# Handing the last stores of two projections to the stages behind them, in a two-layer graph network on one core

## The chip, the cores and the metric

The kernel runs on one core of a Trainium2 chip. Its time is the device time of one execution in microseconds (us), and the median of several runs is compared. Engines are named as in the profile: PE is TensorE (PEld its weight loads), DVE is VectorE, ACT is ScalarE, POOL is GpSimd and SP is SyncE, which only issues DMAs.

## The reference

There are N=1250 nodes with 768 features, 20,000 edges and a loop at each node. Two layers are computed, each with a residual and a layer norm.

```python
# layer 0: x -> x2
x1 = relu(x @ W_ah + b_ah)
for W, a_s, a_d, b in three_convs:          # 4 heads of 192 each: 12 heads in all
    h = (x1 @ W).reshape(N, 4, 192)
    e = leaky_relu((h*a_s).sum(-1)[src] + (h*a_d).sum(-1)[dst], 0.2)
    p = exp(e - segment_max(e, dst)[dst])
    xs.append(relu(segment_sum(p/(segment_sum(p, dst)[dst]+1e-16) * h[src], dst) + b))
x2 = layernorm(x + relu(concat(xs) @ W_out + b_out))

# layer 1: x2 -> out
h   = elu(gat(x2, W1, heads=4, width=512) + b1)
out = layernorm(x2 + gat(h, W2, heads=1, width=768) + b2)
```

## The kernel before

Edges are turned into a dense 1250x1250 matrix of counts (CT), so that an aggregation is a dense product. With u and v, two numbers per destination, the weight of a pair is `min(max(exp(src+u), exp(0.2*src+v)), 1) * CT`. Nodes stand in NT=10 tiles of T=125. The program is eight stages, each a block in which every engine has its own written list of instructions. A block ends when all its engines have ended, with a barrier, and semaphores are cleared behind it.

1. `counts_and_x1`: counts CT, the mask G, and x1, split into two rounded parts (x1T). At its end stands TensorE's `turn_row`, ScalarE's last `mask`.
2. `project` (h of layer 0). VectorE rounds the score weights (wa_hi, wa_lo, L741 and L743); TensorE forms the 24 rows of scores with them (L833, fp32r); ScalarE copies the rows (L788), stores them to DRAM (L791) and fetches the rows of heads 0 and 1 back, each broadcast to 125 partitions (`src_row`, L794). Then TensorE runs 60 tiles of products (L855, six units of ten tiles) and ScalarE keeps each tile in `h_out` (L818), which SP stores to `h_rows` half a unit at a time. Beside it VectorE takes 120 maxima, one for each head and tile (L756), each over a broadcast row; SP fetches the row of a later head into the buffer that has fallen free, in one queue with the stores. From the maxima come u and v of all heads. They are turned by TensorE one after the other (L863), with a copy by ScalarE between and behind (L823), and stored by SP for heads 4 to 11 (L719). SP ends when all stores of h and of u and v have landed. The first head's u, v and h are loaded ahead, into `first_room`.
3. `aggregate_layer0`: six iterations of two heads, ten steps each. A step is two exps by ScalarE (L1002), a maximum and a product with CT by VectorE (L1040, L1045), and ten fp32 products by TensorE (L1089). VectorE also reduces chunks of w2 into score weights in steps 4, 11 and so on; GpSimd loads them (L579, L583). `tail_room`, with the turned results, is allocated here.
4. `project_out_layer0`: ScalarE rounds chunks of W_out (L1770) as they land, VectorE takes the rest (L1808), TensorE multiplies (L1882) and VectorE and ScalarE normalize tile by tile.
5. `project_layer1`: x2 is turned (L1350) and split, products in eight units (L1375), each tile kept as a rounded part by ScalarE (L1268) and the rest by VectorE (L1333) in `h_out`, stored half a unit at a time, tiles 5 to 9 first. SP ends when all stores have landed.
6. `aggregate_layer1`: 120 steps over four heads and three thirds of the destinations. A step is two exps (L1531), maximum and product (L1581, L1583), p rounded (`round_p`, L1503) and its rest (`rest_of_p`, L1573), and 14 products (L1639, L1619). ScalarE first rounds the ones and the negated bias (L1493, L1495). h comes in one load of 0.51 MB per tile. ELU at the end of each third.
7. `project_out_layer1`: chunks of W2 and pieces of the turned result (`f_raw`) are loaded, rounded (L1994, L2002), and multiplied (L2121).
8. `aggregate_last`: 20 steps, with h rounded (L2219) and split (L2248) beside the first ten, then the last layer norm.

```python
            for h in range(2):     # L793, ScalarE in project
                dma_in_two(act, src_row[:, h, :], score_rows[h:h + 1, :].broadcast_to([T, N]), row_in[h])
```

## Time and profile before

| | |
|---|---|
| median of 3 runs | 1965.33 us (1964.57 to 1966.22) |
| the profiled execution | 1964.74 us, span of its instructions 1963.0 us |
| TensorE, VectorE, ScalarE, GpSimd busy | 93%, 74%, 53%, 7% of the span |
| mean granted TensorE clock | 0.968 of full speed |

The span runs from the first to the last instruction. The clock has two levels, 2.4 GHz (1.00 in the views) and 1.2 GHz (0.50). A busy TensorE is not one at its peak, since matrix products are pipelined. Idle time of an engine that doesn't set the end costs nothing.

### The profile page before, as it was taken

Reading aid. Unit: us, or ns where it says so; the run is one execution under the profiler, and the core shown is the slowest. Engines: PE = TensorE matmul, PEld = TensorE weight load, DVE = VectorE, ACT = ScalarE, POOL = GpSimd, SP = SyncE. Lnnn points to the kernel's source line nnn. Section 1 sums busy time; section 2 is a strip of 40 time slices with the busy share of each in tenths; the row PEclk is TensorE's granted clock in tenths of the full one; section 3 lists DMA queues with packets and bytes.
Section 4 is the critical chain, followed back from the end, with each engine's and each line's share of the span. In section 5 each row is a group of like instructions: output and inputs, shape, how many; then the busy total and the mean of one; then the engine's idle time right before and its main releaser. Section 6 shows DMA issues by size and latency. Waiting matters only on the chain. (4 is left out here: it accounts for less than half of the span.)

```text
span 1963.0 us, 30340 instructions
## 1 busy us (share of the span) xinstructions
PE 1817.6 (93%) x11217; PEld 1754.5 (89%) x11217; DVE 1445.3 (74%) x2468; ACT 1034.1 (53%) x1631; POOL 135.3 (7%) x132
## 2 busy tenths in 40 slices
PE   7999899995999999997999899969999996999898
PEld 5777689995999999996999799969999996999798
DVE  7787659998989988984555559447888885346756
ACT  3666522215798898875211322257788874232633
POOL 5011022110000000000011011100000000000000
PEclk8999999997999999997999999989999998999899
DMA  4122154445284344537654566472342406545302
GB/s 123 52 62 67 35 154 138 116 118 133 62 210 100 100 110 101 132 72 197 182 172 147 143 188 192 141 190 66 118 140 68 133 27 183 166 122 129 101 9 79
DMA packets 181465, 234.72 MB, mean 120 GB/s; under 512 B 76102, under 2 KB 154288, under 8 KB 181083
## 3 DMA queue, kind: packets, MB, share of 16 engines
q1 hardware_dynamic: 173215, 205.31, 38.1%
q0 software_dynamic: 7216, 24.91, 4.4%
q10 hardware_dynamic: 902, 2.72, 0.5%
q8 instruction: 85, 1.39, 0.3%
q14 instruction: 47, 0.39, 0.1%
HBM read 167.89 MB, written 65.00 MB: 119 GB/s over the span
## 5 line engine op out<-in xcount | busy, mean ns | idle before, releaser
L1639 PE MATMUL p_o<-p_hi,h_parts 125*128 125x416 f32 (+1 forms) x960 | 282.7, 355 | 22.0 <-DVE p_lo L1573 15.5
L1089 PE MATMUL p_o<-first_room,p 125*125 125x193 f32 x1200 | 202.7, 330 | 13.2 <-DVE p L1045 10.4
L1089 PEld LDWEIGHTS p_o<-first_room,p 125*125 125x125 f32 x1200 | 197.9, 190 | 14.8 <-issue 14.3
L1639 PEld LDWEIGHTS p_o<-p_hi,h_parts 125*128 125x128 f32 x960 | 181.7, 189 | 28.2 <-issue 15.7
L1089 PE MATMUL p_o<-h_in,p 125*125 125x193 f32 x1200 | 198.1, 327 | 0.8 <-ACT res L976 0.8
L1089 PEld LDWEIGHTS p_o<-h_in,p 125*125 125x125 f32 x1200 | 196.0, 188 | 2.3 <-ACT res L976 1.2
L756 DVE CUSTOM_DVE_ANT_0 max_junk<-src_row,G 125x1250 bf16<-125x1250 f32 x120 | 186.2, 1623 | 9.9 <-DMA src_row<-score_rows 9.3
L1040 DVE TENSOR_TENSOR e<-e 125x1250 f32<-125x1250 f32 x120 | 174.3, 1452 | 20.0 <-ACT e L1002 19.9
L855 PE MATMUL p_h<-pw_hi,x1T 128*125 128x384 f32 x720 | 186.4, 340 | 0.0
L1045 DVE SCALAR_TENSOR_TENSOR p<-e,CT 125x1250 f32<-125x1250 f32 x120 | 175.3, 1461 | 4.1
L1375 PE MATMUL p_h<-pw_hi,x2T 128*125 128x256 f32 (+1 forms) x960 | 173.1, 282 | 0.0
L1639 PE MATMUL p_o<-p_lo,h_parts 125*128 125x416 f32 (+1 forms) x480 | 169.9, 354 | 0.0
L1002 ACT ACTIVATE e<-first_room,col 125x1250 f32<-125x1250 f32 x120 | 151.0, 1345 | 7.2 <-DMA b_col<-in_b_gat 4.4
L1002 ACT ACTIVATE e<-uv,col 125x1250 f32<-125x1250 f32 x120 | 149.1, 1349 | 0.9 <-DVE p L1045 0.9
L1375 PEld LDWEIGHTS p_h<-pw_hi,x2T 128*125 128x125 f32 x960 | 146.8, 186 | 0.0
L1375 PE MATMUL p_h<-pw_lo,x2T 128*125 128x256 f32 (+1 forms) x480 | 135.0, 281 | 0.0
L450 PE MATMUL p_count<-src_hot,dst_hot 125*125 125x416 bf16 (+1 forms) x588 | 116.0, 354 | 17.1 <-ACT dst_hot L347 11.3
L855 PEld LDWEIGHTS p_h<-pw_hi,x1T 128*125 128x125 f32 x720 | 130.7, 187 | 0.1
L1882 PE MATMUL p_y<-fw_hi,f_hi 128*125 128x384 f32 x360 | 122.9, 341 | 7.2 <-DVE fw_lo L1808 7.1
L2121 PE MATMUL p_y<-fw_hi,f_hi 128*125 128x386 f32 x320 | 110.6, 346 | 18.1 <-DVE fw_lo L2032 14.6
L450 PEld LDWEIGHTS p_count<-src_hot,dst_hot 125*125 125x125 bf16 x588 | 81.0, 142 | 51.4 <-ACT dst_hot L347 15.5
L278 DVE TENSOR_SCALAR src_hot<-node_no,edge_col 125x1250 bf16<-125x1250 int16 x196 | 106.3, 572 | 27.3 <-PE p_count L450 24.8
(255 smaller groups left out, 3863.3 us busy)
## 6 DMA issues: line engine op xcount, KB each, us to landing
f_raw<-turned SPq DMA_DIRECT2D x40, 500.0 KB, 8.8
h_rows<-h_out SPq DMA_DIRECT2D x32, 560.0 KB
h_parts<-h_rows SPq DMA_DIRECT2D x40, 448.0 KB
turned<-tail_room SPq DMA_DIRECT2D x18, 625.0 KB, 7.3
G<-turned SPq DMA_DIRECT2D x20, 562.5 KB
h_rows<-h_out SPq DMA_DIRECT2D x24, 424.4 KB
first_room<-in_w_gat POOLq DMA_DIRECT2D x36, 192.0 KB, 2.7
first_room<-in_w_gat SPq DMA_DIRECT2D x6, 1152.0 KB
```

The lines of the kernel that those rows point to most:

```text
L278: hot = v.tensor_scalar(src_hot[:, h, :], node_no[:], edge_col[:, 0, h, at], None, ALU.is_equal)
L450: last = nc.tensor.matmul(p_count[:, i, 0:w], dst_hot[:, h, :], src_hot[:, h, a:a + w], start=False, stop=False, skip_group_check=True)
L756: v.tensor_tensor_reduce(out=junk[:, t % 2, :], in0=src_row[:, h % 2, :], in1=G[:, t, :], scale=1.0, scalar=NO_EDGE, op0=ALU.subtract, op1 ...
L855: last = nc.tensor.matmul(p_h[:, (u * NT + t) % 4, 0:width], xp[:, k, at], wp[:, u, k, :], start=(k == 0 and n == 0), stop=(k == KD - 1 an ...
L1002: last = a.activation(e[:, g % RING, kind, :], uv[hh][:, kind, :], ACT.Exp, bias=col_src[kind][:, bass.ds(i * 2 + hh, 1), s])
L1040: v.tensor_tensor(e[:, g % RING, 0, :], e[:, g % RING, 0, :], e[:, g % RING, 1, :], ALU.max).then_inc(more_ready, 1)
L1045: v.scalar_tensor_tensor(p[:, g % RING, :], e[:, g % RING, 0, :], 1.0, CT[:, s, :], ALU.min, ALU.mult).then_inc(p_ready, 1)
L1089: last = nc.tensor.matmul(p_o[:, b, n * 256:n * 256 + C0 + 1], p[:, g % RING, d * T:(d + 1) * T], h_in[hh][:, s, 0:C0 + 1], start=(s == 0 ...
L1375: last = nc.tensor.matmul(p_h[:, n % 4, 0:width], xp[:, k, at], wp[:, q % 2, k, 0:width], start=(k == 0 and j == 0), stop=(k == KD - 1 and ...
L1639: last = nc.tensor.matmul(p_o[:, bank(n, c), 0:w], h[:, s, kind, cols].bitcast(F32R), pp[:, g % RING, 0:w], start=(s == 0 and j == 0), sto ...
L1882: last = nc.tensor.matmul(p_y[:, t % 2, half, 0:CW], fp[:, n % 2, kk, :], wp[:, k, cols], start=(k == 0 and j == 0), stop=(k == KO - 1 and ...
L2121: last = nc.tensor.matmul(p_y[:, t % 2, 0:CW + 2], fp[:, m % 2, kk, :], wp[:, k, :], start=(k == 0 and j == 0), stop=(k == K1 - 1 and j == 2))
```

## The change

- `project`: the score weights are rounded at the end of stage 1 (the room comes from smaller constants there). TensorE itself spreads head 0's score row over 125 partitions, as a product of a column of the identity with the rows, and ScalarE copies it; head 1's row still comes by DMA. `h_out` and `turned_uv` lie in `tail_room`, which is allocated before this stage now. The last half unit of h and the late u and v are not stored here, and nobody waits for landings. u and v are turned in one go.
- `aggregate_layer0`: GpSimd issues the two stores of u and v and the four of h first, then its weight loads. Waits for them stand where their data is first read or their room first written. The wait for the bias moves to where it is used.
- `project_layer1` and `aggregate_layer1`: the same for the last half unit of h (tiles 0 to 4 of the last 256 columns), with four DMAs by GpSimd. An exp in the projection loads the table ahead. The rounding of the ones and of the bias goes behind the first and the fourth step's exps.
- `aggregate_last`: step 0's exps go ahead of the rounding of h, and step 0's p is split at once.
- Identity products by TensorE (`keep_busy`) at ends and starts of stages.

```diff
+def keep_busy(nc, ident, out, n):
+    for _ in range(n):
+        nc.tensor.matmul(out, ident[:, 0:out.shape[0]], ident[:], start=True, stop=True)
 # counts_and_x1: VectorE's end, TensorE's end
+            dve.wait_ge(weighed.summed, weighed.chunks * 2 * weighed.heads)
+            v.tensor_copy(wa_hi[:], wa_flat).then_inc(wa_rounded, 1)
+            dve.wait_ge(wa_rounded, 1)
+            v.tensor_tensor(wa_lo[:], wa_flat, wa_hi[:].bitcast(F32), ALU.subtract)
+            keep_busy(nc, ident, p_count[:, 0, 0:128], 8)
 # project, SyncE
                     for part_no in range(2):
+                        if (i, u, part_no) == (iters - 1, 1, 1):
+                            break
                         wait_apart(sp, h_kept, i * (2 * NT) + (NT * u + NH * (part_no + 1) + 4))
...
-            for u in range(2):
-                sp.wait_ge(h_stored[u], 32 * per * (2 * iters + 1))
-            for kind in range(2):
-                sp.wait_ge(uv_kept, kind + 1)
-                sp.dma_start(core.uv_rows[kind, HG * NT:heads * NT, :], turned_uv[HG * NT:, kind, :]).then_inc(uv_stored, 16)
-            sp.wait_ge(uv_stored, 32)
 # project, ScalarE
             act.dma_start(score_rows[0:R, :], rows[:]).then_inc(rows_stored, 16)
+            act.wait_ge(row_spread, 1)
+            for b, (at, n) in enumerate(CH):
+                last = a.activation(src_row[:, 0, at:at + n], p_r[0:T, b, 0:n], ACT.Copy)
+            last.then_inc(row_in[0], 32)
             act.wait_ge(rows_stored, 16)
-            for h in range(2):
-                dma_in_two(act, src_row[:, h, :], score_rows[h:h + 1, :].broadcast_to([T, N]), row_in[h])
+            dma_in_two(act, src_row[:, 1, :], score_rows[1:2, :].broadcast_to([T, N]), row_in[1])
...
-            for kind in range(2):
-                act.wait_ge(uv_turned, kind + 1)
-                a.activation(turned_uv[:, kind, :], p_s[0:heads * NT, 0:T], ACT.Copy).then_inc(uv_kept, 1)
+            act.wait_ge(uv_turned, 1)
+            a.activation(turned_uv, p_s[0:heads * NT, 0:2 * T].rearrange("p (a q) -> p a q", a=2), ACT.Copy)
 # project, TensorE
-            pe.wait_ge(wa_split, 1)
...
             last.then_inc(rows_turned, 1)
+            for b, (at, n) in enumerate(CH):
+                last = nc.tensor.matmul(p_r[0:T, b, 0:n], ident[0:R, 0:1].broadcast_to([R, T]), rows[:, at:at + n],
+                                        start=True, stop=True)
+            last.then_inc(row_spread, 1)
 # aggregate_layer0: GpSimd, SyncE, ScalarE, TensorE
+            for kind in range(2):
+                pool.dma_start(core.uv_rows[kind, H0 * NT:2 * ITERS * NT, :], uv_last[H0 * NT:, kind, :]).then_inc(core.uv_late, 16)
+            for g in range(2):
+                dma_in_two(pool, h_rows[2 * ITERS - 2 + g, DH:, :].rearrange("(t p) c -> p t c", p=T), h_last[:, 1, :, g, :],
+                           core.h0_late)
...
+            for stored_h in core.h0_stored:
+                sp.wait_ge(stored_h, all_h - 64)
             load(0)
...
+                if i == 0:
+                    sp.wait_ge(core.uv_late, all_uv)
+                if i + 2 == ITERS - 1:
+                    sp.wait_ge(core.h0_stored[0], all_h)
+                    sp.wait_ge(core.h0_late, 64)
                 load(i + 2)
...
-            act.wait_ge(bias_in, 16)
...
+            keep_busy(nc, ident, p_t[:, 0, 0:128], 12)
...
             for c in range(CW):
                 turn(ITERS - 1, c)
+            keep_busy(nc, ident, p_o[:, 0, 0:128], 6)
 # project_out_layer0, TensorE: at the start, and at the end
+            keep_busy(nc, core.ident, p_y[:, 1, 0, 0:128], 7)
...
+            pe.wait_ge(y_left, 2 * (NT - 1))
+            keep_busy(nc, core.ident, p_y[:, NT % 2, 0, 0:128], 28)
 # project_layer1: SyncE, ScalarE
+                    if (q, n) == (UNITS - 1, 1):
+                        break
...
-            for part in range(2):
-                sp.wait_ge(h_stored[part], 64 * UNITS)
...
+                if n == 2 * NT:
+                    a.activation(table_ahead[:], ident[0:T, 0:1], ACT.Exp)
 # aggregate_layer1: GpSimd, SyncE, ScalarE, TensorE
+            for kind in range(2):
+                dma_in_two(pool, h_rows[H1 - 1, 0:DH, kind, HALF1:].rearrange("(t p) c -> p t c", p=T),
+                           h1_last_part(core)[:, :, kind, :], core.h1_late)
...
+            for stored_h in core.h1_stored:
+                sp.wait_ge(stored_h, 64 * (UNITS - 1))
             for s in range(NT):
                 load_h(0, s)
...
-            act.wait_ge(ones_set, 1)
-            a.activation(ones[:], ones_f[:], ACT.Copy).then_inc(ones_set, 1)
-            act.wait_ge(bias_in, 16)
-            a.activation(b_minus[:], b_col[:], ACT.Copy, scale=-1.0).then_inc(bias_in, 16)
-            act.wait_ge(bias_in, 32)
...
+                if g == 0:
+                    act.wait_ge(ones_set, 1)
+                    a.activation(ones[:], ones_f[:], ACT.Copy).then_inc(ones_set, 1)
                 if g:
                     round_p(g - 1)
+                if g == 3:
+                    act.wait_ge(bias_in, 16)
+                    a.activation(b_minus[:], b_col[:], ACT.Copy, scale=-1.0).then_inc(bias_in, 16)
+                    act.wait_ge(bias_in, 32)
...
-            pe.wait_ge(ones_set, 2)
+            keep_busy(nc, core.ident, p_o[:, 7, 0:128], 9)
...
+            pe.wait_ge(left, (ENDS - 1) * CW)
+            keep_busy(nc, core.ident, p_o[:, bank(ENDS - 2, CW - 1), 0:128], 40)
 # project_out_layer1, TensorE's start
+            keep_busy(nc, core.ident, p_y[:, 1, 0:128], 11)
 # aggregate_last: ScalarE, VectorE, TensorE
-                if part == 0:
-                    a.activation(h_hi[:, s, :], h2[:, s, :], ACT.Copy).then_inc(h_hi_done, 1)
+                if part == 0 and s > 1:
+                    round_h(s)
...
-                if g:
+                if g == 0:
+                    round_h(0)
+                    round_h(1)
+                    round_p(0)
+                if g > 1:
                     round_p(g - 1)
...
-                if part == 0:
+                if part == 0 and s:
                     rest_of_h(s)
...
-                if g and s != 1:
+                if g == 0:
+                    rest_of_h(0)
+                    rest_of_p(0)
+                elif s != 1:
                     rest_of_p(g - 1)
                 add(g)
-                if s == 1:
+                if g == NT + 1:
                     rest_of_p(g - 1)
...
+            keep_busy(nc, core.ident, p_o[:, 7, 0:128], 16)
```

## Rows read from the trace of the kernel before

**Rows 1.** The page: busy time of the engines, and two of its groups.
```profile
PE 1817.6 (93%) x11217; PEld 1754.5 (89%) x11217; DVE 1445.3 (74%) x2468; ACT 1034.1 (53%) x1631; POOL 135.3 (7%) x132
...
L1089 PE MATMUL p_o<-h_in,p 125*125 125x193 f32 x1200 | 198.1, 327 | 0.8 <-ACT res L976 0.8
...
L756 DVE CUSTOM_DVE_ANT_0 max_junk<-src_row,G 125x1250 bf16<-125x1250 f32 x120 | 186.2, 1623 | 9.9 <-DMA src_row<-score_rows 9.3
```

**Rows 2.** Waits of TensorE over the span: us in total, times, longest.
```profile
PE p_o L1639 <- DVE p_lo L1573: 15.5, 1, 15.5
PE p_y L2121 <- DVE fw_lo L2032: 14.6, 1, 14.6
...
PE p_o L1089 <- DVE p L1045: 10.4, 1, 10.4
```

**Rows 3.** Timeline of the first projection's start: start, length, idle time before.
```profile
251.44 2.13 ACT L785 ACTIVATE pw_hi<-first_room 128x2304 fp32r<-128x2304 f32 x1 [1.90 <-DMA first_room<-in_w_gat]
...
254.91 1.31 ACT L788 ACTIVATE score_rows_in<-p_r 24x418 f32<-24x418 f32 x3 [1.34 <-PE p_r L833]
...
256.27 1.27 PE L838 MATMUL p_s<-ident,score_rows_in 24*125 24x24 f32 x10 [1.40 <-ACT score_rows_in L788]
...
261.29 1.91 ACTq L93 DMA_DIRECT2D src_row<-score_rows  x4
...
269.42 1.46 DVE L756 CUSTOM_DVE_ANT_0 max_junk<-src_row,G 125x1250 bf16<-125x1250 f32 x1 [9.29 <-DMA src_row<-score_rows]
```

**Rows 4.** Timeline from the projection's end into the first aggregation, all engines.
```profile
448.62 0.34 PE L855 MATMUL p_h<-pw_hi,x1T 128*125 128x384 f32 x1
...
458.82 0.19 DVE L769 SCALAR_TENSOR_TENSOR col<-dst_now,tmp 125x40 f32<-125x40 f32 x1
...
463.26 0.36 SPq L925 DMA_DIRECT2D b_col<-in_b_gat  x1
...
465.14 6.25 ACT L1002 ACTIVATE e<-first_room,col 125x1250 f32<-125x1250 f32 x5 [4.41 <-DMA b_col<-in_b_gat]
...
484.22 0.72 POOL L583 DMA_DIRECT2D wa_by_w<-in_w  x1 [18.29 <-DVE wa L597]
```

**Rows 5.** Windows where TensorE starts: busy us (instructions) by engine, granted clock, DMA.
```profile
470.80:475.80 5.00, 5.00 (x16) 5.00 (x17) 4.93 (x4) 5.00 (x5) 0.00 (x0) 0.50 1.01 283
475.90:480.90 5.00, 5.00 (x33) 5.00 (x32) 4.93 (x5) 5.00 (x5) 0.00 (x0) 1.00 0.72 159
...
1304.70:1308.70 4.00, 4.00 (x12) 3.81 (x13) 3.90 (x8) 4.00 (x9) 0.00 (x0) 0.50 1.05 261
...
1837.60:1841.20 3.60, 3.59 (x17) 3.60 (x18) 3.56 (x5) 3.11 (x5) 0.00 (x0) 0.50 0.38 109
```

**Rows 6.** Timeline from layer 1's projection into its aggregation.
```profile
1289.61 0.42 DVE L1333 TENSOR_TENSOR h_out<-p_h,h_out 125x256 fp32r<-125x256 f32 x1 [1.70 <-ACT h_out L1268]
...
1297.04 0.36 SPq L1467 DMA_DIRECT2D b_col<-in_b  x1
...
1299.16 1.28 ACT L1531 ACT_TABLE_LOAD   x1
...
1303.94 0.59 DVE L1573 TENSOR_TENSOR p_lo<-e,p_hi 125x418 fp32r<-125x418 f32 x1
```

**Rows 7.** Timeline of ScalarE at the start of the two output projections.
```profile
916.04 0.85 ACT L1770 ACTIVATE fw_hi<-G 128x768 fp32r<-128x768 f32 x1 [1.86 <-DMA G<-in_w_out]
...
1658.50 1.04 ACT L2002 ACTIVATE f_hi<-f_raw 128x1000 fp32r<-128x1000 f32 x1 [4.87 <-DMA f_raw<-turned]
```

**Rows 8.** Timeline of the last aggregation's start.
```profile
1829.52 0.84 ACT L2219 ACTIVATE h_hi_l<-h 125x768 fp32r<-125x768 f32 x1 [8.87 <-PEq L69]
1830.27 1.51 ACT L2223 ACTIVATE G<-x_ring,col 125x625 f32<-125x625 f32 x2
...
1831.81 0.81 DVE L2314 TENSOR_TENSOR G<-G 125x625 f32<-125x625 f32 x1 [0.46 <-ACT G L2223]
...
1837.61 0.97 PE L2347 MATMUL p_ol<-h_hi_l,p_hi_l 125*125 125x256 f32 x3 [9.62 <-DVE p_lo_l L2252]
```

More of the change, by code:

```diff
@@ L217, in _ @@
                                pattern=[[1, NT]], channel_multiplier=-1).then_inc(later_ready, 1)
-            for m in (band, ident_b, zeros_b):
-                pool.memset(m[:], 0.0).then_inc(consts, 1)
-            pool.wait_ge(consts, 6)
-            pool.affine_select(out=ident_b[:], in_=ident_b[:], compare_op=ALU.not_equal, fill=1.0, base=0,
-                               pattern=[[-1, T]], channel_multiplier=1).then_inc(consts, 1)
+            pool.memset(band[:], 0.0).then_inc(consts, 1)
+            pool.wait_ge(consts, 4)
             pool.affine_select(out=band[:], in_=band[:], compare_op=ALU.not_equal, fill=1.0, base=N - T,
@@ L251, in _ @@
             step(v.scalar_tensor_tensor(meets[:, 0, :], least, tile_lo[:, 1:2], meets[:, 0, :], ALU.is_lt, ALU.mult))
-            step(v.scalar_tensor_tensor(meets[:, 1, :], run_no_i[:], float(-ER), meets[:, 0, :], ALU.add, ALU.mult))
-            step(v.scalar_tensor_tensor(meets[:, 2, :], run_no_i[:], 1.0, meets[:, 0, :], ALU.add, ALU.mult))
+            step(v.scalar_tensor_tensor(meets[:, 1, :], run_no_i, float(-ER), meets[:, 0, :], ALU.add, ALU.mult))
+            step(v.scalar_tensor_tensor(meets[:, 2, :], run_no_i, 1.0, meets[:, 0, :], ALU.add, ALU.mult))
             step(v.tensor_reduce(out=range_f[:, 2:3], in_=meets[:, 1, :], axis=AX.X, op=ALU.min))
@@ L452, in count @@
                         last.then_inc(hot_free, 1)
-                nc.tensor.matmul(p_count[:, 0, 0:2], zeros_b[:], band[:, 0:2], start=False, stop=True,
+                nc.tensor.matmul(p_count[:, 0, 0:2], zeros_b, band[:, 0:2], start=False, stop=True,
                                  skip_group_check=True).then_inc(counted, 1)
@@ L653, in project @@
         h_kept = sem("h_kept")
-        h_stored = [sem(f"h_stored{u}") for u in range(2)]
+        h_stored = core.h0_stored
         ones_set = sem("ones_set")
@@ L787, in _ @@
             for b, (at, n) in enumerate(CH):
-                last = a.activation(rows[:, at:at + n], p_r[:, b, 0:n], ACT.Copy)
+                last = a.activation(rows[:, at:at + n], p_r[0:R, b, 0:n], ACT.Copy)
             last.then_inc(rows_kept, 1)
@@ L981, in keep @@
             def keep(i, c):
+                if i == 0 and c == 0:
+                    act.wait_ge(bias_in, 16)
+                    act.wait_ge(core.uv_late, all_uv)
+                    act.wait_ge(core.h0_stored[0], all_h)
+                    act.wait_ge(core.h0_late, 64)
                 act.wait_ge(turned, i * CW + (c + 1 + CW))
@@ L1157, in project_layer1 @@
         h_split = sem("h_split")
-        h_stored = [sem(f"h_stored{u}") for u in range(2)]
+        h_stored = core.h1_stored
         uv_turned = sem("uv_turned")
@@ L1443, in bank, with _ @@
             return (n * PER + c) % 8
+        UNITS = 2 * H1
+        @block.gpsimd
+        def _(pool):
+            for kind in range(2):
+                dma_in_two(pool, h_rows[H1 - 1, 0:DH, kind, HALF1:].rearrange("(t p) c -> p t c", p=T),
+                           h1_last_part(core)[:, :, kind, :], core.h1_late)
         @block.sync
@@ L1510, in elu_exp @@
                 act.wait_ge(left, k)
+                if n == 0 and c == 0:
+                    act.wait_ge(core.h1_late, 64)
                 if n >= 2:
@@ L2421, in gnn_two_layers @@
             core.first_h_in = sem0("first_h_in")
+            core.h0_stored = [sem0(f"h0_stored{u}") for u in range(2)]
+            core.uv_late = sem0("uv_late")
+            core.h0_late = sem0("h0_late")
             with ExitStack() as inner:
@@ L2437, in gnn_two_layers @@
             tail.close()
-            with ExitStack() as innermost:
-                sb2 = core.tools(innermost)[0]
-                x2T = [sb2(f"x2T{i}", [128, KD, N], F32R) for i in range(2)]
-                project_layer1(nc, core, x2T, x2_rows, w1, core.wa1, h1_rows, score_rows, cols[0:2], *cols[2:4])
-            w2_halves = w2.rearrange("(u g) r c -> u (g r) c", u=2)
-            with ExitStack() as ahead:
+            with ExitStack() as ahead:
+                core.tail_room = ahead.enter_context(nc.sbuf_tensor("tail_room1", [128, TAIL1], F32, side="right"))
+                core.h1_stored = [sem1(f"h1_stored{u}") for u in range(2)]
+                core.h1_late = sem1("h1_late")
+                with ExitStack() as innermost:
+                    sb2 = core.tools(innermost)[0]
+                    x2T = [sb2(f"x2T{i}", [128, KD, N], F32R) for i in range(2)]
+                    project_layer1(nc, core, x2T, x2_rows, w1, core.wa1, h1_rows, score_rows, cols[0:2], *cols[2:4])
+                w2_halves = w2.rearrange("(u g) r c -> u (g r) c", u=2)
                 core.f_raw = ahead.enter_context(nc.sbuf_tensor("f_raw", [128, 2, K1 // 2, T], F32, side="right"))
                 core.w_first = ahead.enter_context(nc.sbuf_tensor("fw_first", [128, K1 // 2, D // 2], F32, side="right"))
-                core.tail_room = ahead.enter_context(nc.sbuf_tensor("tail_room1", [128, TAIL1], F32, side="right"))
                 aggregate_layer1(nc, core, h1_rows, cols[0:2], b1, turned1, w2_halves)
```

82 lines of the change are left out of this document (46 added, 36 removed).

## The prediction, made before the changed kernel was run

> **What bounds the kernel now.** I read the page first. TensorE is busy for 93% of the span, VectorE for 74% [rows 1]: time is to be won where TensorE stands still or runs at half clock. The waits of TensorE, sorted by length, come next. Eight of them, from 4.6 to 15.5 us, happen once each, at or near a border between two stages; three stand here [rows 2]. Then I took the timeline at each border and asked what ends last.
>
> In the first projection that is not TensorE. Its last product starts at 448.62, while VectorE ends its chain of maxima at 459.01 [rows 4]. That chain starts at 269.42 behind 9.3 us of waiting for the first broadcast row of scores, and 9.9 us is all the idle time its 120 maxima have [rows 1, 3]. So it moves as a block: a start x earlier is an end x earlier.
>
> **The change part by part.** The sum is made in the profiled execution: span 1963.0, its time 1964.74. The median of the runs is 1965.33, and I subtract the sum from that.
>
> *First row by TensorE.* ScalarE rounds the second weights until 251.44+2.13=253.57 [rows 3]. TensorE's score products, freed from a wait for VectorE at the stage's start, are done by about then. So: three copies 1.31, to 254.9; ten transposes 1.27, to 256.2 [rows 3]; then the new spread, three fp32 products of 418 columns, which run as two passes each (L1089 stands with 2,400 instructions for 1,200 products). A pass of 193 columns takes 198.1/1200=0.165 us [rows 1], and twice that at half clock, where 5 us hold 16 passes for 33 [rows 5]; times 418/193 and six passes that is 2.1 or 4.3 us. Three copies of 125 partitions: at least the 1.31 of the copies of 24, I take 1.4. With the hand-overs the maxima start at 259.9 to 262.1; I take the middle, 261.0, a shift of 8.4, so the chain ends at 450.6. TensorE's own products start at 258.3 to 260.5, up to 3 us later than now, and end at 448.3 to 451.9, beside the chain. The other rows are issued when a buffer falls free; a row is then wanted ten maxima of 1.46 us later, and the first two took 8.1 us from their issue at 261.29 [rows 3]. That slack hides them.
>
> *Last stores handed over.* From the chain's end to the next stage's first issue it takes 4.25 us, 459.01 to 463.26 [rows 4], for two transposes, two copies, a store of u and v, its landing and the barrier. After: two transposes without a copy between (0.6 with the hand-over), one copy (0.4, as one of the three above), 1.0 for barrier and clearing. That is 452.6 for 463.26: 10.6 gained with the 8.4.
>
> *GpSimd's six issues.* They stand ahead of the weight loads that VectorE first reduces in step 4, some 18 us into the stage. An issue cost 0.72 us beside running VectorE products [rows 4]; a store of h has 2.2 times as many pieces as that load, so 0.72 to 1.6 each, 4.3 to 10 us in all, and the load lands in time. Cost 0, hidden by four steps. The Trainium skill (SBUF — State Buffer, 🔬 SBUF: two separate sides) speaks against handing DMAs to GpSimd: while VectorE runs certain two-port copies, GpSimd can't write descriptors, and a DMA goes from about 0.62 to 3.1 us. By that, as an estimate, six issues take some 19 us and VectorE would wait a few us once. The 0.72 us row does not show it for the products that run here.
>
> *First aggregation, start.* The first exps no longer wait for the bias: 465.14 [rows 4] for 463.5, 1.6. Then 5.66 us of exp, maximum and product remain to TensorE's start at 470.80 [rows 5]. TensorE's first 5 us ran at half clock: 2.5 lost [rows 5]. The stage is TensorE's from its first step (20 passes, 3.3 us, against two VectorE products of 1.46), so clock is time here. The 12 identity products are 24 passes of 128 columns, 0.11 us at full and 0.22 at half by the same rows: 2.6 or 5.2 us, under the cover of those 5.66. They leave up to 3 us of idle before the real products, so I take half of the 2.5: 1.3 (0 to 2.5). This border: 10.6+1.6+1.3=13.5.
>
> *Output projection of layer 0.* Its start at half clock returns nothing: the ninth weight chunk reaches ScalarE only at 916.04 [rows 7] and TensorE about 1.8 later (0.85 for the rounding, as much for the rest), when it is about there now; a faster TensorE waits for the DMA. The six products behind the last turn may pass the barrier: -0.1 (0 to -0.5).
>
> *Projection of layer 1, start.* ScalarE and VectorE round and subtract in a chain that TensorE's transposes only follow: 0.2.
>
> *Second aggregation, start.* The last subtraction ends at 1290.03, the next stage begins at 1297.04 [rows 6]. Without the landing of the last stores 1.0 of barrier is left: 6.0 gained. Then the table load of 1.28 goes [rows 6] (into the projection, on a ScalarE that waits for TensorE at every tile), with the rounding of the ones and the wait for the bias. Exps could begin at 1297.35 and p_lo be ready at 1301.8; now 1303.94+0.59=1304.5: 2.7. Its first 4 us at half clock [rows 5] cost up to 2.0. Against that stands a transfer that used to be over: 1.28 MB of stores now share the engines with ten loads of 0.51 MB, and the engines are already full at 261 GB/s [rows 5]. A load takes 2.0 us of it, TensorE's step 2.7. If the store goes first it costs 1.28/0.261=4.9 us, of which the loads' lead hides 1.3 by the third step: up to 3.6. The larger pieces of the loads should get more than half: I take 1.8 for contention, and 0.4 of the clock. The Trainium skill (DMA: Bandwidth & Descriptors, Issuing engines are not separate DMA queues) says that transfers issued by different engines interleave on the same 16 engines; by that GpSimd's queue gives no room of its own, and the sum would carry the full 3.6. This border: 6.0+2.7+0.4-1.8=7.3 (4.5 to 10.7).
>
> *Output projection of layer 1.* Its start at half clock returns nothing either: the third piece is held by a landing at 1658.50 [rows 7], and two faster pieces wait longer for it. 0. The 40 products end 9 to 10 us after the last real one, under the 11 us to the next stage.
>
> *Last aggregation.* Exps first, h rounded behind. From 1829.52: exps 1.51, VectorE's two products 0.81 each [rows 8], p rounded 0.7, then h_lo 0.95 and p_lo 0.8 (by their columns): TensorE starts at 1834.4 for 1837.61 [rows 8]. Step 1 now waits for p_lo(1), behind add(1) and the products of step 2: 1840.8. Before, 17 of step 0's 45 products took 3.6 us at half clock [rows 5], and step 1 began near 1844.4. Gain 3.6 with the clock held, 3.0 without: 3.4.
>
> Sum: 13.5-0.1+0.2+7.3+3.4=24.3. 1965.3-24.3=1941.0.
>
> **Rivals.**
> - *The identity products don't hold the clock.* For: idle stretches of 2 us and more remain between them and the first real products. Against: they halve every stretch. Price 1.3+0.4+0.4: 1943.1.
> - *The late stores take the loads' place.* Full 3.6 for 1.8, and as much again if the loads of the first aggregation are held: 1942.8 to 1945.
> - *The maxima start no earlier,* because the next row is late: all 8.4 lost, 1949.4. For: the first two rows took 8.1 us together. Against: only one is needed now, with ten maxima of cover.
> - *Slower.* GpSimd's issues in the first aggregation. At 8 us each the weight loads land after 50 us, VectorE stands at its first reduction from 18 us on, TensorE behind it, and some 30 us go. It decides from about 7 us each (42 us less 18 eat the 24); at 9 us each it would be 1971. Against: 0.72 us [rows 4].
>
> **How the numbers follow.** Forecast 0.60; clock 0.13; stores 0.13; maxima 0.07; slower 0.03; 0.04 for more than all the bounds. Bounds summed: best 1.1+2.5+3.4+0.5 more than mine, 1933.5; worst -1.5-1.8-2.8-0.9 and the maxima, 1950. The range of 1932 to 1950 leaves out the slower rival and the rest. No change can't be told from differences under 0.2% (3.9 us): faster 0.95, same 0.02, slower 0.03.
>
> **What would show it.** The first maximum a good us behind the score copies instead of 9; the first aggregation beginning near 452.6; no table load in the second, its first product within 5 us of the stage's start or held by h_parts; a wait of TensorE of about 1 us before step 1 of the last stage; longer waits for the DMA in both output projections. I am wrong if VectorE idles between maxima, if TensorE's products end far behind the chain, or if one GpSimd issue is long.

## The result, and the profile after

The change makes the kernel faster. The median of 4 runs is 1947.15 us (1945.75 to 1952.59), against 1965.78 us (1964.57 to 1969.89) in 4 runs of the kernel before: a ratio of 0.9902, 95% interval 0.9882 to 0.9921. The profiled execution has a span of 1944.2 us, for 1963.0 before. That is 18.8 us less, where 24.3 were forecast.

The page first. TensorE is busy for 95% of the span and not 93%, with 280 more instructions (274 passes of identity products and the six of the spread), so that a part of the 95% is no work; the idle time ahead of the maxima has fallen from 9.9 us [rows 1] to 3.2.

```profile
PE 1848.0 (95%) x11497; PEld 1783.2 (92%) x11497; DVE 1445.9 (74%) x2468; ACT 1033.4 (53%) x1634; POOL 140.8 (7%) x139
...
L1118 PE MATMUL p_o<-h_in,p 125*125 125x193 f32 x1200 | 199.8, 329 | 2.8 <-ACT res L1000 2.8
...
L761 DVE CUSTOM_DVE_ANT_0 max_junk<-src_row,G 125x1250 bf16<-125x1250 f32 x120 | 184.9, 1612 | 3.2 <-ACT src_row L799 1.6
```

The waits of TensorE (total, times, longest). The three long ones of [rows 2] are gone from the list, in part only because identity products now stand in them. What is left at the borders is under 3 us each. The wait for ScalarE's `res` inside the first aggregation has grown: in the kernel before its longest was 1.0 us, the first of these rows, and now it is 2.8.

```profile
PE p_o L1089 <- ACT res L976: 3.7, 4, 1.0
```

```profile
PE p_o L1118 <- ACT res L1000: 5.7, 4, 2.8
...
PE p_s L844 <- ACT score_rows_in L793: 1.6, 1, 1.6
```

The start of the first projection, which answers to [rows 3]. The first maximum starts at 262.07 instead of 269.42, behind ScalarE's copy of the spread row and no longer behind a DMA. But the six spreading passes took 4.51 us, all at half clock.

```profile
250.17 10.10 POOL L742 TENSOR_TENSOR pw_lo<-first_room,pw_hi 128x2304 fp32r<-128x2304 f32 x2 [9.07 <-ACT pw_hi L790]
...
254.39 1.67 PE L844 MATMUL p_s<-ident,score_rows_in 24*125 24x24 f32 x10 [1.61 <-ACT score_rows_in L793]
...
255.89 4.51 PE L847 MATMUL p_r<-score_rows_in,ident 24*125 24x418 f32 x6
...
256.54 3.82 DVE L752 COPY col<-score 125x120 f32<-125x120 f32 x1
...
260.33 0.68 PE L865 MATMUL p_h<-pw_hi,x1T 128*125 128x384 f32 x1
...
262.07 1.46 DVE L761 CUSTOM_DVE_ANT_0 max_junk<-src_row,G 125x1250 bf16<-125x1250 f32 x1 [1.58 <-ACT src_row L799]
```

```profile
core 0: us, PE busy (x) PEld busy (x) DVE busy (x) ACT busy (x) POOL busy (x), PEclk, DMA share, GB/s
255.90:260.30 4.40, 4.40 (x7) 1.77 (x7) 4.17 (x3) 0.00 (x0) 4.38 (x1) 0.50 0.83 246
497.50:500.80 3.30, 3.30 (x10) 3.30 (x11) 3.27 (x3) 3.30 (x9) 0.00 (x0) 0.50 1.03 259
1101.70:1105.20 3.50, 1.51 (x6) 1.08 (x6) 3.23 (x5) 1.95 (x5) 0.00 (x0) 0.50 1.02 296
```

The columns of these windows are those of [rows 5]; the value ahead of the DMA share is the granted clock, 0.50 in all three. From the projection's end into the aggregation, for [rows 4]: VectorE is done with the last of the columns at 451.35, but TensorE's own products now last until 452.57, so it is TensorE that ends the stage.

```profile
451.16 0.19 DVE L774 SCALAR_TENSOR_TENSOR col<-dst_now,tmp 125x40 f32<-125x40 f32 x1
...
452.24 0.33 PE L865 MATMUL p_h<-pw_hi,x1T 128*125 128x384 f32 x1
...
453.00 0.37 ACT L830 ACTIVATE tail_room<-p_s 120x250 f32<-120x250 f32 x1
454.16 0.36 SPq L943 DMA_DIRECT2D b_col<-in_b_gat  x1
...
454.63 8.71 ACT L1030 ACTIVATE e<-first_room,col 125x1250 f32<-125x1250 f32 x7 [1.25 <-DVEq L1048]
454.65 1.06 POOL L928 DMA_DIRECT2D uv_rows<-tail_room  x2 [51.12 <-POOLq L70]
...
455.70 2.80 POOL L94 DMA_DIRECT2D h_rows<-tail_room  x4
```

TensorE's and VectorE's rows in the first aggregation show the new wait. TensorE runs the first head's ten steps (200 passes) in 34.40 us, then stands for 2.78 us. VectorE waits 0.88 us for the first weight chunk in step 4; at step 11 two reductions stand ahead of the sums that the divisors are made from.

```profile
460.29 34.40 PE L1118 MATMUL p_o<-first_room,p 125*125 125x193 f32 x200 [2.82 <-issue]
497.47 2.91 PE L1118 MATMUL p_o<-h_in,p 125*125 125x193 f32 x8 [2.78 <-ACT res L1000]
```

```profile
472.53 0.96 DVE L614 CUSTOM_DVE_ANT_1 wa_by_junk<-wa_by_w,wa_by_a 128x768 bf16<-128x768 f32 x1 [0.88 <-DMA wa_by_w<-in_w]
...
494.37 0.95 DVE L614 CUSTOM_DVE_ANT_1 wa_by_junk<-wa_by_w,wa_by_a 128x768 bf16<-128x768 f32 x1
...
496.12 0.16 DVE L1057 TENSOR_SCALAR sums<-p_o 125x4 f32<-125x4 f32 x1
```

Layer 1, for [rows 6]: from the last subtraction to the first issue it takes 0.88 us for 7.01. No table is loaded in the new stage, and `p_lo` is ready 4.2 us into it. TensorE is then held by the load of h, once at its first and once at its third step.

```profile
1283.50 0.42 DVE L1366 TENSOR_TENSOR tail_room<-p_h,tail_room 125x256 fp32r<-125x256 f32 x1 [1.69 <-ACT tail_room L1298]
1284.80 0.36 SPq L1509 DMA_DIRECT2D b_col<-in_b  x1
...
1285.30 2.83 POOL L94 DMA_DIRECT2D h_rows<-tail_room  x4 [35.44 <-POOLq L70]
...
1288.44 0.59 DVE L1623 TENSOR_TENSOR p_lo<-e,p_hi 125x418 fp32r<-125x418 f32 x1
...
1289.66 0.72 PE L1692 MATMUL p_o<-p_hi,h_parts 125*128 125x418 f32 x1 [2.57 <-DMA h_parts<-h_rows]
...
1295.22 0.46 PE L1672 MATMUL p_o<-p_hi,ones 125*128 125x418 f32 x1 [1.24 <-DMA h_parts<-h_rows]
```

To see where the time came from, I cut the span of each execution at the same work: the last product of the counts, the first product of the first aggregation, and the last real product of each stage behind it. Gains are in us against the profiled execution of the kernel before. The last column gives the lowest and highest gain over the nine later kernels that keep the change's identity products, less those whose edit is in that stage.

| part | forecast | after | others |
|---|---|---|---|
| counts | 0 | 0.84 | 0.3 to 2.4 |
| projection, up to the first product of the aggregation | 12.2 | 9.66 | 8.4 to 9.9 |
| first aggregation | 1.3 | -2.63 | -2.8 to -1.7 |
| output projection of layer 0 | -0.1 | -0.57 | -4.5 to 0.0 |
| projection of layer 1 | 0.2 | -1.21 | -2.5 to -1.1 |
| second aggregation with its border | 7.3 | 8.03 | 5.5 to 8.8 |
| output projection of layer 1 | 0 | 1.07 | -1.9 to 2.5 |
| last aggregation | 3.4 | 3.64 | 1.6 to 3.6 |
| sum | 24.3 | 18.8 | |

### The profile page after: what moved, and what is told of

Its sections match the earlier page's. It is cut to its first block and busy times, and to the rows that moved or that the text cites. A ratio compares the mean times of both kernels' runs of the same rounds, so it can differ in the third digit from the quotient of the medians.

```text
span 1944.2 us, 30898 instructions
## 1 busy us (share of the span) xinstructions
PE 1848.0 (95%) x11497; PEld 1783.2 (92%) x11497; DVE 1445.9 (74%) x2468; ACT 1033.4 (53%) x1634; POOL 140.8 (7%) x139
## 5 line engine op out<-in xcount | busy, mean ns | idle before, releaser
L1692 PEld LDWEIGHTS p_o<-p_hi,h_parts 125*128 125x128 f32 x960 | 181.6, 189 | 14.9 <-DVE z L1611 10.2
L865 PE MATMUL p_h<-pw_lo,x1T 128*125 128x384 f32 x360 | 122.4, 340 | 0.0
```

The source lines that it names most:

```text
L865: last = nc.tensor.matmul(p_h[:, (u * NT + t) % 4, 0:width], xp[:, k, at], wp[:, u, k, :], start=(k == 0 and n == 0), stop=(k == KD - 1 an ...
L1692: last = nc.tensor.matmul(p_o[:, bank(n, c), 0:w], h[:, s, kind, cols].bitcast(F32R), pp[:, g % RING, 0:w], start=(s == 0 and j == 0), sto ...
```

## Experiments

Each kernel is the changed one with the edit shown; in a diff, `...` or a comment stands for lines that are not printed. A profile is of one execution, and a median of four or five runs still moves by some 2 us, so a verdict on a part is read from the parts of the profile.

**The changed kernel again**

> The changed kernel once more, for the spread of its stages between executions. If the stages between the borders repeat to 0.3 us and only the half-clock stretches behind waits differ, its parts are as before but for those: 1945 to 1949.

Measured: 1948.21 us (1945.20 to 1950.76), ratio 0.990 (0.9885 to 0.9914), span 1946.5. The projection gains 9.80, the first aggregation -2.55, the second 8.03, as before. The others moved by 0.8, 1.2 and 0.5 us. So the two parts in which most of the forecast is missing repeat. What happens inside the aggregation does not repeat: the weight chunk came 1.4 us later, TensorE waited 3.56 us at the second head, and the clock did not fall there.

```profile
473.96 0.96 DVE L614 CUSTOM_DVE_ANT_1 wa_by_junk<-wa_by_w,wa_by_a 128x768 bf16<-128x768 f32 x1 [2.46 <-DMA wa_by_w<-in_w]
...
498.90 0.40 PE L1118 MATMUL p_o<-h_in,p 125*125 125x193 f32 x1 [3.56 <-ACT res L1000]
```

**Divisors ahead of the reductions**

```diff
-                    if (i * STEPS + g) % 7 == 4 and ...:   # weighed.reduce
-                    if g == NT + 1:
-                        divisors(i, 0)
+                    if g == NT + 1:
+                        divisors(i, 0)
+                    if (i * STEPS + g) % 7 == 4 and ...:   # weighed.reduce
```

> Theory (VectorE's written order makes the wait at the second head of the first aggregation: the divisors stand behind two reductions of 0.95 us, and the idle time then costs a step at half clock): the sums come 1.75 us sooner, TensorE's wait of 2.78 us shrinks to about 1, the next step takes 3.5 us for 5.17; 3.5 us together, 1943.6. Rival (the half clock there has nothing to do with the length of that wait): the step still takes 5.2 us, 1.8 us gained, 1945.4. Rival (the first weight chunk's late landing is the cause): the wait keeps over 2 us, 1946.5 or more.

Measured: 1945.94 us (1944.63 to 1953.64), ratio 0.9906 (0.9889 to 0.9922). The median doesn't resolve it, the profile does: the aggregation as a whole loses 0.78 and not 2.63. The first sums are formed at 494.85, before TensorE has ended the head (496.77), the second head starts at once, and no clock falls. This is the theory's mechanism, but not its 3.5 us: 1.85 are gained, for at the third head TensorE now waits 1.01 us for VectorE's next divisors, a wait that the changed kernel does not have there. The profiled span of 1952.0 is longer all the same. The loss lies elsewhere: the second aggregation began with 10.2 us at half clock for 3.4, the output projection of layer 0 lost 1.6 more, and the last two stages gained 3.0 and 2.0 less.

```profile
494.85 0.16 DVE L1057 TENSOR_SCALAR sums<-p_o 125x4 f32<-125x4 f32 x1
...
497.12 0.96 DVE L614 CUSTOM_DVE_ANT_1 wa_by_junk<-wa_by_w,wa_by_a 128x768 bf16<-128x768 f32 x1
...
529.31 0.15 DVE L1057 TENSOR_SCALAR sums<-p_o 125x4 f32<-125x4 f32 x1
...
530.66 1.05 PE L1118 MATMUL p_o<-first_room,p 125*125 125x193 f32 x5 [1.01 <-ACT res L1000]
```

```profile
496.61 3.64 PE L1118 MATMUL p_o<-h_in,p 125*125 125x193 f32 x20
```

**Weight loads ahead of the late stores**

```diff
-            # GpSimd: two stores of u and v, four of h
             weighed.loads(pool, ...)      # first vector, first two chunks
+            # here the six stores, then the rest of the loads
```

> GpSimd issues its first loads of weights ahead of the six late stores. Theory (the stores only cost VectorE its 0.88 us of waiting for the first chunk): that wait goes, TensorE's wait at the second head shrinks from 2.78 to 1.9 us, and 1.0 us is gained if the clock still falls there, 2.6 if it doesn't: 1946.2 to 1944.5. Rival (what comes late is the traffic of this stage's own loads, whatever the order of issue): no change, 1947.1.

Measured: 1949.16 us (1943.82 to 1951.69), ratio 0.992 (0.9896 to 0.9944). VectorE's wait for the chunk is gone, and the aggregation loses 1.67 for 2.63: 0.96 gained, as the theory has it for a clock that still falls. It did fall (it was down from 496.2 to 499.6). TensorE ran its first head wholly at full clock, came sooner and waited 3.30 us. The profiled execution lost 4.45 us in the output projection of layer 0, with a wait of 4.1 us for a weight chunk and 6.8 us at half clock behind it; against stages that vary so much the median says nothing on this edit.

```profile
496.07 4.20 PE L1122 MATMUL p_o<-h_in,p 125*125 125x193 f32 x14 [3.30 <-ACT res L1004]
```

**No identity products**

```diff
 def keep_busy(nc, ident, out, n):
-    for _ in range(n):
-        nc.tensor.matmul(out, ident[:, 0:out.shape[0]], ident[:], start=True, stop=True)
+    return
```

> All identity products left out. By the prediction's clock terms (1.3, 0.4 and 0.4) it takes 2.1 us more than with them: 1949.3. Rival from the changed kernel's trace (held over the border of the second projection, the clock falls 1.6 us into it instead, and one step of the first aggregation is at half clock behind a wait in either case): 1 us or less, 1948. Rival (the stages' starts are mostly half clock without them, at up to 2 us each at five places): 1952 or more.

Measured: 1943.99 us (1940.40 to 1946.69), ratio 0.9892 (0.9872 to 0.9912). All three expectations were of a longer time; it was not longer. The half-clock stretches between 200 and 1925 us do grow, from 47.8 to 95.6 us in all. What counts is how much of TensorE's real work lies in them, and that grows from 39.9 to 56.7 us only. In the first aggregation those 5 us are at half clock again, but TensorE then comes later to the second head, waits 1.42 us and keeps its clock: the stage loses 0.91 for 2.63.

```profile
458.70:463.70 5.00, 5.00 (x16) 5.00 (x17) 4.93 (x4) 5.00 (x5) 0.34 (x1) 0.50 1.05 297
```

```profile
458.66 35.67 PE L1117 MATMUL p_o<-first_room,p 125*125 125x193 f32 x200 [7.54 <-DVE p L1072]
495.75 3.50 PE L1117 MATMUL p_o<-h_in,p 125*125 125x193 f32 x20 [1.42 <-ACT res L999]
```

**First row by DMA again**

```diff
-            act.wait_ge(row_spread, 1)
-            # three copies from p_r to src_row[:, 0]
             act.wait_ge(rows_stored, 16)
-            dma_in_two(act, src_row[:, 1, :], ...)
+            for h in range(2):
+                dma_in_two(act, src_row[:, h, :], ...)
-            # TensorE: the three products that spread the row
```

> The first broadcast row by DMA again. Theory (the maxima are a rigid chain and the row's 6.5 us pass on, less the 1.2 us by which TensorE's products outlast them in the changed kernel): the first maximum at about 268.6 instead of 262.1, the next stage's first issue 5.3 us later, 1952.4. Rival (TensorE's products set the end of that stage, and starting them 3 us sooner makes up for much of it): under 3 us, 1950 at most.

Measured: 1951.55 us (1951.18 to 1956.06), ratio 0.9936 (0.9919 to 0.9952), some 3 to 4 us more than with the spread. The projection gains 6.37 for 9.66, so the spread is worth 3.3 us of the 8.4 forecast. A part of those came without it: the first maximum started at 266.33, 2.4 us sooner than in [rows 3] beside the 0.7 of the earlier counts. The score weights rounded a stage ahead are the likely cause; no run has that change alone. TensorE's products ended at 448.65, before the maxima, and didn't set the end. The next stage issued at 457.59, 3.4 us later than in the changed kernel and not the theory's 5.3, so the rival is the nearer one on the mechanism, and that the median lies near the theory's 1952.4 is chance.

```profile
266.33 1.46 DVE L761 CUSTOM_DVE_ANT_0 max_junk<-src_row,G 125x1250 bf16<-125x1250 f32 x1 [5.74 <-DMA src_row<-score_rows]
```

**Layer 0's late stores waited for**

```diff
-                        if (i, u, part_no) == (iters - 1, 1, 1):
-                            break
+            # SyncE, at the end of project, behind the last half unit of h: u and v
+            for u in range(2):
+                sp.wait_ge(h_stored[u], 32 * per * (2 * iters + 1))
+            for kind in range(2):
+                sp.dma_start(core.uv_rows[kind, HG * NT:heads * NT, :], turned_uv[...]).then_inc(core.uv_late, 16)
+            sp.wait_ge(core.uv_late, 32)
-            # GpSimd, in aggregate_layer0: the same stores
```

> The last half unit of h and the late u and v of layer 0 are stored and waited for in the projection again. By the prediction's step (store, landing and copy of u and v are some 2 of the 10.6 us): the next stage's first issue 2 us later, 1949. Rival (with TensorE's last product now at the very end, the last half unit of h, 0.96 MB, lands after u and v and holds the stage): 5 to 6 us later, 1952.7. Rival (the first aggregation waits at its second head anyway, so the loads and VectorE's first reduction gain what is lost): 1948 or less.

Measured: 1954.23 us (1950.96 to 1955.67), ratio 0.9932 (0.9909 to 0.9956), 6 to 7 us more than the changed kernel: the first rival's. The stores of h, issued at 448.50, hold u and v until 454.58, and the next stage issues at 457.53. From the last maximum to VectorE's first operation of the aggregation it takes 13.2 us for 6.8, and 9.65 in the kernel before, where the maxima outlasted those stores. So the gain of the row isn't there to be added up without the hand-over: here the spread ran at full clock and the maxima started 10.4 us sooner than in the kernel before (8.1 beside the earlier counts), and yet the projection gains only 4.91. With the hand-over and without the row it gains 6.37, with both 9.66. Both single kernels keep the smaller edits of the change (score weights ahead, one turn for u and v, the bias waited for later), so 4.91 and 6.37 are not the prices of the two parts by themselves.

```profile
448.11 0.19 DVE L779 SCALAR_TENSOR_TENSOR col<-dst_now,tmp 125x40 f32<-125x40 f32 x1
...
448.50 2.52 SPq L94 DMA_DIRECT2D h_rows<-tail_room  x4
...
454.58 0.79 SPq L733 DMA_DIRECT2D uv_rows<-tail_room  x2
457.53 0.36 SPq L943 DMA_DIRECT2D b_col<-in_b_gat  x1
```

**Layer 1's late stores waited for**

```diff
-                    if (q, n) == (UNITS - 1, 1):
-                        break
+            # SyncE, at the end of project_layer1
+            for part in range(2):
+                sp.wait_ge(h_stored[part], 64 * UNITS)
-            # GpSimd, in aggregate_layer1: the four stores
```

> The last half unit of layer 1 is stored and waited for in its projection again. Theory (the landing wait is worth 6.1 us, and the handed-over stores delay the loads by little, about 1 us): from the last subtraction to the next stage's first issue 7.0 us instead of 0.9, loads of h 2.0 us apart from the first, 5 us lost in all, 1952. Rival (the handed-over stores take the loads' place in full, 3.6 us): 2.5 us lost, 1949.6.

Measured: 1952.19 us (1948.30 to 1955.28), ratio 0.9916 (0.9888 to 0.9944), as the theory has it. The border grows from 0.88 to 6.91 us, and the second aggregation with it gains 4.87 for 8.03: 6.0 lost and 2.9 had back. Of these, 1.2 us are the wait at the third step, which is gone, and some 1.5 the half clock, which ended at 1296.5 here, ahead of the first product (1297.87).

```profile
1285.72 0.42 DVE L1366 TENSOR_TENSOR tail_room<-p_h,tail_room 125x256 fp32r<-125x256 f32 x1 [1.69 <-ACT tail_room L1298]
1286.17 2.82 SPq L94 DMA_DIRECT2D h_rows<-tail_room  x4
1293.05 0.36 SPq L1502 DMA_DIRECT2D b_col<-in_b  x1
```

**Layer 1's late stores behind the loads**

```diff
         def _(pool):
+            pool.wait_ge(h_loaded[9], 32)
             for kind in range(2):
                 dma_in_two(pool, h_rows[...], h1_last_part(core)[:, :, kind, :], core.h1_late)
```

> GpSimd issues the four handed-over stores of layer 1 only when the ten loads of h have landed. Theory (TensorE's waits for h_parts at its first and third step, 0.6 and 1.2 us, are the stores' doing): both shorter, the tenth load 5 us sooner, up to 1.8 us gained, 1945.4. Rival (the loads' own rate and the exps set these steps): the same waits, 1947.1.

Measured: 1945.51 us (1942.13 to 1950.56), ratio 0.9888 (0.9858 to 0.9918). The wait at the third step is gone, and the second tile of h landed at 1291.66 instead of 1295.18. Yet the stage gains 7.91 for 8.03. Here the half clock lasted 6.8 us, so that the third step's products still ran at 0.55 us each: TensorE was as late without the wait. That the median lies near the theory's 1945.4 is therefore no gain of this edit. The first wait did not shrink (2.89 us in the row, for 2.57): these four stores are not what makes it.

```profile
1289.83 0.72 PE L1692 MATMUL p_o<-p_hi,h_parts 125*128 125x418 f32 x1 [2.89 <-DMA h_parts<-h_rows]
...
1294.87 0.55 PE L1672 MATMUL p_o<-p_hi,ones 125*128 125x418 f32 x1
```

**Identity products in the wait for the copies**

```diff
             last.then_inc(rows_summed, 1)
+            keep_busy(nc, ident, p_h[:, 3, 0:128], 6)
             pe.wait_ge(rows_kept, 1)
```

> The changed kernel with six identity products in TensorE's 1.6 us of waiting for the copies of the scores. Theory (the clock falls in that wait; the three spreading products take 4.5 us for 2.3 and TensorE's products outlast the maxima): spread 2.3 us, first maximum 2.2 us sooner, the next stage's first issue 2.5 to 3 us sooner, 1944.3. Rival (the fall has its cause further back, at the stage's start): the half-clock stretch lies there all the same, 1947.

Measured: 1945.20 us (1941.87 to 1951.85), ratio 0.9892 (0.9873 to 0.9911), span 1941.5. The projection gains 11.16 for 9.66. The spread took 2.87 us, at full clock until 256.2, and the first maximum started at 259.45. Neither expectation is met whole: the half-clock stretch is still there, only 1.1 us later and 6.8 us long for 10.2, and TensorE still waited 2.09 us, for the six products fill 1.5 of it only. Nor is the gain surely the edit's, since the spread ran wholly at full clock in two kernels that don't have it. The theory gave 2.2 us more by the clock; 1.5 came, because another thing is late next. VectorE's copy of 120 columns takes 4.25 us and ends with GpSimd's subtraction of the weights (249.21 to 259.32).

```profile
249.21 10.11 POOL L742 TENSOR_TENSOR pw_lo<-first_room,pw_hi 128x2304 fp32r<-128x2304 f32 x2 [9.32 <-ACT pw_hi L790]
...
254.52 2.87 PE L848 MATMUL p_r<-score_rows_in,ident 24*125 24x418 f32 x6
...
255.16 4.25 DVE L752 COPY col<-score 125x120 f32<-125x120 f32 x1
...
259.45 1.45 DVE L761 CUSTOM_DVE_ANT_0 max_junk<-src_row,G 125x1250 bf16<-125x1250 f32 x1
```

**Both orders, without identity products**

The edits of the divisors, the weight loads and the identity products together.

> No identity products, the divisors ahead of the reductions, and the weight loads ahead of the late stores. Theory (the second head's wait and a clock held at the start take turns: without identity products the first step runs at half clock and TensorE comes later to a wait that is 0.7 us beyond the steady one): 1 us less than without identity products alone, 1943. Rival (the identity products are worth their 2 us once that wait is gone): 1945 to 1946, no better than with them.

Measured: 1944.59 us (1941.75 to 1947.38), ratio 0.9886 (0.9861 to 0.991), beside 1943.99 without the orders: not told apart by the medians. Its profiled execution has a span of 1940.1, of which some 3 us come from a projection whose spread ran at full clock (2.34 us) with nothing done for it. The first aggregation loses 0.65 us, 0.26 less than with the old order.

**All of it, with and without the change's identity products**

The divisors, the weight loads, layer 1's stores behind the loads and the six new identity products together; in the second kernel `keep_busy` returns at once, and only those six are left.

> The changed kernel with these six, the divisors and the weight loads ahead, and layer 1's late stores behind its loads. By the traces so far 2.7 and 3.5 us are gained at two places: 1941. Rival (the next late thing takes over at the second head): 1944.

> The same orders and the six new identity products, but none of the change's own. Theory (the change's own identity products only move half-clock stretches from ahead of a stage's work into it, or into a wait, and give nothing on the whole): the same time as with them, 1941. Rival (they are worth the 2 us of the prediction once the other waits are gone): 2 us or more behind the kernel with them.

Measured, on one chip with the changed kernel's 1948.21: with them 1942.93 us (1936.16 to 1943.74), ratio 0.9864 (0.9845 to 0.9884); without 1941.46 (1941.04 to 1942.45), ratio 0.9869 (0.9854 to 0.9884). Both are 5 to 7 us faster than the changed kernel, with intervals that don't touch its own, and not told apart from each other. In the first aggregation the identity products are now worth what was forecast: 0.80 us gained for 0.68 lost, 1.5 us between them. In the projection it is the other way round: without them it gained 13.04, with them 11.13. There TensorE's wait ahead of the spread was only 0.20 us, and the half clock came behind the spread (258.4 to 261.8, for 255.6 to 262.4). In these two profiles the two cancel. That leaving them out does this isn't shown: of the other kernels without them one gained 13.07 and one 10.19. I would keep the one without: its executions also lay closer together.

## Why the prediction was right, and where it was off

The forecast of 1941.0 was 6 us too low, the range of 1932 to 1950 held the time, and faster was right. In the profiled execution the sum is short by 5.5 us. Point by point:

- *First row by TensorE, shift 8.4.* It was 7.35, or 6.5 less the 0.84 by which this whole execution was early. The mechanism was right. The step that failed is "I take the middle": the spread took 4.51 us, above the 4.3 at half clock, and in the eight other profiles that leave that stretch as it is 4.5 in five, 3.92 in one and 2.34, the full clock's, in two. So the two ends of the estimate were two states of the clock, and most executions lay at one of them. The clock was down from 255.10 on, 0.7 us behind TensorE's wait of 1.6 us. That the wait is the cause is not shown: with a wait of 0.20 us it fell too, at 258.4, behind the spread.
- *TensorE's products end beside the chain.* They ended at 452.57, outside the 448.3 to 451.9, and TensorE, not VectorE, set the end, 1.2 us later. Of this some 0.7 us are the half clock, which went on for 5 us into them (until 265.3). The rest is their length: they took 191.5 us at the least in all 14 profiles, and in two of the three kernels with the spread wholly at full clock they still ended 0.5 us behind the maxima's chain (in the third 0.4 ahead). The first issue came at 454.16 for 452.6. The first exps stood 0.47 us behind it, for 1.88 before: 1.4 us gained for 1.6.
- *GpSimd's six issues cost 0.* The issues did take 0.53 to 0.82 us. What was missed is the transfer: with the stores ahead of it the chunk landed at 472.39, and VectorE waited 0.88 us (2.46 in the second execution). With the loads first, or with no late stores, it did not wait; nor did it in the kernel with the row by DMA, so the stores ahead don't always cost this wait. The Trainium skill (SBUF — State Buffer, 🔬 SBUF: two separate sides) gives 3.1 us for a DMA that GpSimd issues beside a VectorE copy. No issue here took that long; VectorE ran its maxima and products beside them, and no such copy.
- *The stage is TensorE's from its first step; clock 1.3.* This is the step that failed most. TensorE's part was right (4.99 us for the first step, 5.99 before). But VectorE needs 38.9 us from its first maximum of exps to the first divisors (37.9 where it has no wait for the chunk), and TensorE only 34.4 for the ten steps, so it waited out at the second head what the clock had given. It was 10.51 us ahead of the kernel before at its first product, 9.54 at the second head's first, and 7.87 behind that step, at half clock again: 7.03 beside the early start, for 13.5 forecast. With the divisors ahead TensorE kept 10.3 us behind that step, and lost 1.2 of them at the third head: VectorE's side then bounds that place.
- *Output projection -0.1, layer 1's start 0.2.* Measured -0.57 and -1.21. Held up to the border, the clock fell 1.6 us into the projection of layer 1 instead, and was down until 1108.4, through its first products (from 1106.87); in the kernel before it was up again 3 us ahead of them (1110.7 for 1113.70). The identity products are not to blame: the three kernels without them were at half clock through the same products, until 1102.8 to 1106.0, and lose 1.2 to 1.8 us here too. Why the kernel before got by is open.
- *Second aggregation 7.3.* Measured 8.03: the landing 6.13 (forecast 6.0), `p_lo` 3.26 sooner in the stage (2.7), TensorE's waits for the loads of its first and third tile 0.49 and 1.24 more (1.8), and 0.4 left for the clock (0.4). Every term held.
- *Output projection of layer 1, 0.* Measured 1.07, but -1.9 to 2.5 over the other executions.
- *Last aggregation 3.4.* Measured 3.64, TensorE's start 3.1 us and step 1 another 0.5 sooner. In five of ten executions 2 us of it were lost again, in a half-clock stretch of 10.2 us around the wait at the second part, which lasts 3.4 or 6.8 us in the other five.

Two sums of the prediction are off without touching the forecast: GpSimd issues of 9 us each give 54 less 18, so 1977 (1971 is the figure for 8 us), and the worst case of 1950 does not hold the lost maxima too: its four terms give 1948, the maxima by themselves 1949.4, and both together 1956.

Of the rivals, *the identity products don't hold the clock* was nearest and still wrong about the mechanism. They hold it; it doesn't pay. They took 48 us of half clock away and gave 17 us of work back its full clock, worth 8 us if all of it were TensorE's alone. The medians show no such gain. These are starts of stages, and in those that were traced a DMA, a copy or VectorE's order set the time. *The late stores take the loads' place* was seen in the landings (second tile 5.6 us behind the first, 1.9 with the stores behind the loads) but cost no more than the 1.7 us above. *The maxima start no earlier* and *slower* did not happen.

What stays open is why a stretch at half clock is 3.4 us long in one execution and 6.8 or 10.2 in another at the same place. The Trainium skill (TensorE: Matmul & The Clock Gate, Part 1) says that the number of products at half clock at a kernel's start differs from run to run of the same kernel. These traces agree for places further in: the changed kernel's stretch in the last aggregation was 3.4 us long in one execution and 6.8 in the other.

## What to carry to other kernels

When a stage begins with its engines in step, ask which of them is last at the first point where they meet again, not only which is busier per step: here VectorE's written order, two side jobs ahead of the one result that another engine waits for, ate all that the held clock had gained TensorE, and more. Two edits that shorten the same end are not added up but tried as a pair, since each may lay bare what the other hides. And products that only hold the clock are worth what the real work behind them gains, after the next wait, and not the length of the half-clock stretch that they remove.

## What the runs showed of the hardware

- TensorE's clock fell at the end of a wait of 2.78 us (497.44) and 0.7 us behind one of 1.6 us (255.10), but not at one of 3.56 us (498.90 in the second execution). The stretches at half clock were 3.4, 6.8 or 10.2 us long at one and the same place in different executions. Much of what executions of one stage differed by, where I traced it, lies there.
- A VectorE copy between places in SBUF was held by a running GpSimd operation: 120 columns took 3.82 us beside GpSimd's subtraction and ended with it (260.36 and 260.27), 4.25 us in another kernel; in all 14 profiles the copy ended within 0.1 us of the subtraction. The Trainium skill (SBUF — State Buffer, 🔬 SBUF: two separate sides) has this as a lock on a shared pair of ports that the first comer holds for the whole instruction; the traces agree. The first maximum followed this copy at once in three of the five kernels whose spread took 3.3 us or less; in the other two the row itself was 0.3 to 0.4 us later.
- Four stores of 1.28 MB in all, issued within the first 2.8 us of a stage, moved the second tile of h from 1.9 to 5.6 us behind the first (3.4 in the second execution), and the fourth from 6.0 to 10.0 (10.4).
